# Decision trees: key rows begin at query chunk 22 in place of 26, value rows share every second step with a chunk, leaf weights asked for ahead of slot rows

## The chip, the core and the metric

The kernel runs on one core of a Trainium2 chip. The metric is device time in microseconds; the kernel before takes 2354.35 us, the median of three executions (2353.2 to 2354.74). TensorE (PE in the rows; PEld is its weight load), VectorE (DVE), ScalarE (ACT), GpSimd (POOL) and SyncE (SP) each run their own instructions in order and meet only through semaphores. SyncE issues most DMAs; GpSimd issues the indirect ones.

## What is computed

A decoder of 12 layers over 64 sequences of 64 tokens, 128 features each. The change touches the third layer alone, an attention whose queries, keys and values come out of three decision trees. Each tree has 4 levels and 16 leaves, and each leaf is a small two-layer network (128 to 64 to 128):

```python
def _fff(x, node_w, node_b, w1, b1, w2, b2):
    ...
    cur = jnp.zeros((N,), jnp.int32)
    for _ in range(DEPTH):
        pw = node_w[cur]
        score = jnp.einsum('nd,nd->n', xf, pw) + node_b[cur]
        cur = 2 * cur + 1 + (score >= 0).astype(jnp.int32)
    leaf = cur - N_NODES
    sel = jax.nn.one_hot(leaf, N_LEAVES, dtype=xf.dtype)
    hidden_all = jax.nn.relu(jnp.einsum('nd,ldh->lnh', xf, w1) + b1[:, None, :])
    hidden = hidden_all * sel.T[:, :, None]
    out = jnp.einsum('lnh,lho->no', hidden, w2) + sel @ b2
...
attn = jax.nn.softmax(jnp.einsum('bqd,bkd->bqk', q, k) * scale, axis=-1)
return jnp.einsum('bqk,bkd->bqd', attn, v)
```

## The kernel before

The layer is the function `trees`. Its 4096 tokens are 32 tiles of 128, or 8 groups (`g`) of 512.

**Queries** are computed densely: all 16 leaves for every token, the wrong ones switched off. The work is 64 *chunks*, `m` = 0 to 63: chunk `m` is two leaves of group `m // 8`. `make_hidden(m)` (lines 2057, 2058) makes its hidden part in one of two PSUM banks, ScalarE's `relu` (1948) takes it to SBUF, `add_leaf(m)` (2067) multiplies by the second matrix and sums the group in PSUM; the first chunk of a group also multiplies in the biases (2065). After eight chunks ScalarE takes the group's query (`take_q`, 1952). `turn_leaves(b)` (2032) transposes the leaf choices of two groups; the first is made ahead, the others at chunks given by `leaves_at`.

**Keys and values** are computed sparsely. GpSimd scatters the tokens into a table in memory, sorted by leaf (1742): 32 indirect DMAs for the keys, then 32 for the values. The table has 47 tiles of 128 slots for each, every tile of one leaf. Four tiles make a *quad*; quads 0 to 11 are key rows, 12 to 23 value rows (quads 11 and 23 have three tiles). SyncE loads a quad's slots into one of 5 buffers (`load_slots`, 1692) and the weights of each tile's leaf into one of 16 (`load_weights`, 1685), whose address it reads from a table (1684). For quad `m` TensorE transposes the slots (`turn_rows`, 2078), VectorE copies them (1859), TensorE makes the hidden part (`hide_rows`, 2087), ScalarE takes it with bias and relu (1959), TensorE makes the output (`yield_rows`, 2097), VectorE copies it (1866) and SyncE stores it (`store_rows`, 1698).

GpSimd then fetches the rows back to their tokens with 32 indirect DMAs for keys (1751), four to a group, group 0 once quad 11 is stored, group `g` once the transpose of group `g - 2` is done, and 32 for values (1763), once all quads are stored and all key groups fetched; it waits after every second value group. TensorE transposes the keys of group `g` (`turn_k`, 2105), makes scores (`score`, 2116), VectorE and ScalarE the softmax's numerators, TensorE transposes them (`turn_weights`, 2126) and multiplies by the values (`weigh`, 2140), and VectorE adds the result to x (`update`, 1887). The next layer starts when all engines are done.

**The order** is written out by hand, the same on each engine. Chunks run alone up to a fixed one, `ROWS_FROM`. From there on a counter of steps, `i`, starts at 0, and step `i` holds a chunk as long as there are any, the transpose of quad `i`, the hidden part of quad `i - 1`, the output of quad `i - 2`, and whatever the tables `keys_at`, `scores_at`, `weights_at` and `values_at` place there. On TensorE:

```python
for m in range(LAST + ROWS_FROM + 1):
    i = m - ROWS_FROM
    ...
    if m < NM:
        add_leaf(m)
    if rows_at(i):
        turn_rows(i)
    if rows_at(i - 1):
        hide_rows(i - 1)
    if rows_at(i - 2):
        yield_rows(i - 2)
```

SyncE has its own loop: it loads the weights of quads 0 to 3 and the slots of quads 0 to 4 ahead, and then, in iteration `m`, stores quad `m`, loads the slots of quad `m + 5` and the weights of quad `m + 4`.

## Time and profile before

| what | value |
|---|---|
| time, median of 3 executions | 2354.35 us (2353.2 to 2354.74) |
| span of the profiled execution, first to last instruction | 2356.9 us |
| busy: TensorE, VectorE, ScalarE, GpSimd | 75%, 57%, 47%, 32% of the span |
| the stage `trees` in that execution | 395.9 to 725.6 us; the next layer starts at 729.0 |
| row steps (step 0 to the output of quad 23) | 507.9 to 661.5 us |

The table's three times belong to executions of their own, the span to the profiled one; what lies around the span (start and end of the program) is not in it. The busy shares are means over twelve layers with different limits, and say nothing of this stage; what it waits for is read in its own stretch, engine by engine, since all are in order. Of the rows below, those of a timeline begin with the start and the duration in us, and end, in brackets, with the time that the engine was idle before and what ended it ("remote": a semaphore whose update the profile ties to no instruction close by). "SPq" is SyncE's queue.

### The profile page before, as it was taken

What the parts mean: (1) busy time and instruction counts of PE and PEld (TensorE: products, weight loads), DVE (VectorE), ACT (ScalarE), POOL (GpSimd) and SP (SyncE); (2) the same over time, 40 slices, a digit from 0 to 9 for tenths busy, and PEclk for the clock granted to TensorE, in tenths of its full rate; (3) what the DMA queues carried; (4) which work ended last, traced back from release to release, by engine and by line L of the source; (5) the groups of instructions that cost most, each with busy time, mean ns of one, the idle gap of its engine ahead of it and who ended that gap; (6) DMA issues with size and microseconds to landing.
All of it is one profiled execution on the core that took longest, in us unless ns stands there. A gap on an engine that the chain in (4) does not pass through costs nothing. (4 is left out here: it accounts for less than half of the span.)

```text
span 2356.9 us, 39525 instructions
## 1 busy us (share of the span) xinstructions
PE 1774.8 (75%) x14484; PEld 1215.4 (52%) x14484; DVE 1337.8 (57%) x3646; ACT 1099.5 (47%) x2273; POOL 746.9 (32%) x718
## 2 busy tenths in 40 slices
PE   3887553999895996767999386887788868743994
PEld 1555432435543664644798253565555535542774
DVE  3897587502123774654343365885369969862223
ACT  4775531223243775733344243774357657610441
POOL 1223201360354331146255002330223232165453
PEclk9888885798896998877999697998979969955997
DMA  4111361125623301102376200000000010011224
GB/s 158 83 83 82 104 235 45 49 75 150 161 70 132 124 2 50 37 30 85 110 238 201 75 1 27 28 20 10 3 1 2 2 37 28 11 49 60 62 81 138
DMA packets 145170, 173.18 MB, mean 73 GB/s; under 512 B 21073, under 2 KB 120593, under 8 KB 144049
## 3 DMA queue, kind: packets, MB, share of 16 engines
q1 hardware_dynamic: 125252, 129.09, 17.7%
q0 software_dynamic: 13248, 28.21, 3.6%
q10 hardware_dynamic: 6480, 13.37, 1.5%
q8 instruction: 117, 1.92, 0.3%
q14 instruction: 73, 0.60, 0.1%
HBM read 126.84 MB, written 79.05 MB: 87 GB/s over the span
## 5 line engine op out<-in xcount | busy, mean ns | idle before, releaser
L1154 PE MATMUL a_AV<-a_vx,a_pT 128*64 128x18 f32 (+1 forms) x3072 | 115.1, 224 | 33.0 <-DVE a_two L824 15.3
L1154 PEld LDWEIGHTS a_AV<-a_vx,a_pT 128*64 128x64 f32 x3072 | 105.9, 146 | 62.2 <-issue 28.6
L1016 ACT ACTIVATE a_e<-a_e 128x512 f32<-128x512 f32 x192 | 110.2, 622 | 58.7 <-DVE a_e L846 58.5
L1141 PE MATMUL a_TP<-ident,a_e 128*128 128x128 f32 x768 | 108.0, 285 | 20.0 <-ACT a_e L1016 19.4
L1021 ACT COPY a_pT<-a_TP 128x512 f32<-128x512 f32 x192 | 103.4, 588 | 39.6 <-PE a_TP L1141 39.4
L846 DVE TENSOR_TENSOR a_e<-a_S,a_mx 128x1024 f32<-128x1024 f32 x96 | 117.3, 1222 | 2.9
L1141 PEld LDWEIGHTS a_TP<-ident,a_e 128*128 128x128 f32 x768 | 89.2, 146 | 57.6 <-ACT a_e L1016 48.3
L1130 PE MATMUL a_S<-a_kbd,a_qT 64*64 64x512 f32 x768 | 113.8, 668 | 0.9 <-issue 0.6
L3620 POOL DMA_INDIRECT f_back<-f_ys,f_row x78 | 74.7, 957 | 97.5 <-DVE f_ys L3709 85.6
L3126 POOL DMA_INDIRECT f_back<-f_ys,f_row x80 | 76.6, 957 | 87.1 <-DVE f_ys L3287 66.9
L3759 ACT ACTIVATE f_h<-f_H,f_wt 128x256 f32<-128x256 f32 x156 | 65.2, 473 | 83.5 <-PE f_H L3835 83.5
L843 DVE TENSOR_REDUCE a_mx<-a_S 128x16 f32<-128x1024 f32 x66 | 80.8, 1224 | 40.6 <-PE a_S L1130 39.4
L3352 ACT ACTIVATE f_h<-f_H,f_b 128x512 f32<-128x512 f32 (+1 forms) x96 | 56.5, 615 | 85.4 <-PE f_H L3445 78.6
L1948 ACT ACTIVATE f_h<-f_H,f_b 128x512 f32<-128x512 f32 x64 | 44.0, 687 | 103.1 <-PE f_H L2058 85.5
L1154 PE MATMUL x_AV<-x_vx,x_pT 128*64 128x18 f32 x2048 | 74.2, 215 | 23.7 <-ACT x_pT L1021 17.0
L843 DVE TENSOR_REDUCE x_mx<-x_S 128x16 f32<-128x1024 f32 x64 | 78.1, 1221 | 24.3 <-PE x_S L1130 24.0
L681 POOL TENSOR_TENSOR a_kbd<-a_kT,a_mask 128x512 f32<-128x512 f32 x64 | 64.5, 1039 | 81.1 <-ACT a_kT L991 81.1
L1154 PEld LDWEIGHTS x_AV<-x_vx,x_pT 128*64 128x64 f32 x2048 | 69.0, 142 | 37.2 <-issue 24.9
L1141 PEld LDWEIGHTS x_TP<-ident,x_e 128*128 128x128 f32 x512 | 58.4, 146 | 55.0 <-ACT x_e L1016 45.3
L1141 PE MATMUL x_TP<-ident,x_e 128*128 128x128 f32 x512 | 74.7, 290 | 15.5 <-ACT x_e L1016 15.4
L999 ACT ACTIVATE a_kbd<-a_kT,a_mask 128x512 f32<-128x512 f32 x128 | 85.6, 723 | 0.4
L671 POOL TENSOR_TENSOR a_rstd<-a_var,neghalf 128x4 f32<-128x4 f32 x24 | 24.3, 1014 | 187.7 <-DVE a_var L747 117.8
(544 smaller groups left out, 4731.4 us busy)
## 6 DMA issues: line engine op xcount, KB each, us to landing
f_wt<-in_f_ew SPq DMA_DIRECT2D x39, 584.0 KB
f_slots<-in_blank SPq DMA_DIRECT2D x1, 18576.0 KB
f_wt<-in_f_leaf SPq DMA_DIRECT2D x94, 98.0 KB, 2.0
f_xs<-f_slots SPq DMA_DIRECT2D x47, 144.0 KB
memory_x_k<-w_stage ACTq DMA_DIRECT2D x24, 256.0 KB, 3.2
f_slots<-in_blank SPq DMA_DIRECT2D x1, 5760.0 KB
f_xs<-leaf_slots SPq DMA_DIRECT2D x22, 256.0 KB
leaf_out<-f_ys SPq DMA_DIRECT2D x22, 256.0 KB
```

What stands on the lines that cost most here:

```text
L681: last = pool.tensor_tensor(kbd[:, n % 2, b:b + 2, 0:4, :], bc(kv[:, b:b + 2, :], 2, shape), mask8[:, 0:4].unsqueeze(1).unsqueeze(3).to_br ...
L843: return v.tensor_reduce(mx[:, i % 2, :], unit(i), AX.X, ALU.max)
L846: v.tensor_tensor(e[:, i % 2, :, :], unit(i), bc(mx[:, i % 2, :], 2, [P, NH, SL]), ALU.subtract).then_inc(shifted.sem, 1)
L999: last = act.activation(kbd[:, n % 2, :, h, :], keys(n).rearrange("p (b j) -> p b j", j=SL), ACT.Copy, scale=mask8[:, h:h + 1])
L1016: act.activation(eh, eh, ACT.Exp).then_inc(weights.sem, 1)
L1021: act.copy(pT[:, 4 * n:4 * n + 4, :], TP[:, n, :].rearrange("p (a b) -> p a b", a=4)).then_inc(pT_half.sem, 1)
L1130: last = pe.matmul(S[64 * c:64 * c + 64, i % 2, r, :], qT[rows, g % 2, SL * b:SL * b + SL], kbd[rows, g % 2, b, :, :], start=True, stop=True)
L1141: last = pe.transpose(TP[:, half, P * n:P * n + P], ev[:, 4 * half + n, :], k.ident[:, :])
L1154: last = pe.matmul(AV[64 * c:64 * c + 64, 2 * hp * W1:2 * (hp + 1) * W1], pT[:, hp, 64 * c:64 * c + 64], vx[:, g % 2, t, c, 2 * hp:2 * hp ...
L3126: pool.indirect_dma_start(out=back[:, :], out_offset=bass.IndirectOffsetOnAxis(ap=row[:, i % RR, t:t + 1], axis=0), in_=ys[:, i % RY, t, : ...
L3620: pool.indirect_dma_start(out=back[:, :], out_offset=bass.IndirectOffsetOnAxis(ap=row[:, i % RR, t:t + 1], axis=0), in_=ys[:, i % RY, t, : ...
L3759: act.activation(h[:, i % 2, c, 0:P * n], hid(i, c, n), ACT.Gelu_apprx_tanh, bias=weights(i)[2][:, c:c + 1])\
```

## The change

```diff
-    ROWS_FROM = 26
-    LAST = 46
-    leaves_at = {8: 1, 14: 2, 20: 3}
-    keys_at = {max(16 + 2 * g, 8 * g - 15): g for g in range(NG)}
-    scores_at = {25 + 2 * g if g < NG - 1 else 42: g for g in range(NG)}
-    weights_at = {27 + 2 * g if g < NG - 1 else 44: g for g in range(NG)}
-    values_at = {31 + 2 * g: g for g in range(NG)}
+    ROWS_FROM = 22
+    LAST = 52
+    leaves_at = {6: 1, 11: 2, 16: 3}
+    keys_at = {i: g for g, i in enumerate((17, 19, 21, 23, 24, 26, 34, 42))}
+    scores_at = {i: g for g, i in enumerate((24, 26, 28, 30, 32, 34, 42, 49))}
+    weights_at = {i: g for g, i in enumerate((26, 28, 30, 32, 34, 36, 44, 51))}
+    values_at = {i: g for g, i in enumerate((32, 34, 36, 38, 40, 43, 46, 52))}
     rows_at = lambda m: 0 <= m < 2 * NQ
+
+    def chunk_at(i):
+        if i < NQ:
+            return ROWS_FROM + i
+        if i < 2 * NQ + 2:
+            return None if (i - NQ) % 2 else ROWS_FROM + NQ + (i - NQ) // 2
+        m = ROWS_FROM + NQ + (NQ + 2) // 2 + i - 2 * NQ - 2
+        return m if m < NM else None
...
             for m in range(2 * NQ):
                 store_rows(m)
-                if m + RXS == NQ:
-                    sp.wait_ge(scattered[1].sem, scattered[1].after(NT - 1))
-                if rows_at(m + RXS):
+                if rows_at(m + RXS) and not NQ - RXS <= m < NQ - 3:
+                    if m == NQ - 3:
+                        sp.wait_ge(scattered[1].sem, scattered[1].after(NT - 1))
+                        for n in range(NQ, NQ + RXS - 3):
+                            load_slots(n)
                     load_slots(m + RXS)
```

`NQ` is 12, `RXS` 5 and `NM` 64. The loops of TensorE and ScalarE now run over the step `i` from -22 to 52 and take their chunk from `chunk_at(i)`: chunk `22 + i` up to step 11, chunks 34 to 40 at the even steps 12 to 24, none at the odd steps 13 to 25, and chunks 41 to 63 at steps 26 to 48.

On SyncE, around iterations 7 to 9, before (the store is that of quad 7; the wait for the value scatter is the second semaphore of the slot load):

```order
L1685 DMA f_wt<-in_f_leaf 128x196
L1698 DMA leaf_out<-f_ys 128x4x128 [waits f0_ys_ready]
L1692 DMA f_xs<-leaf_slots 128x4x128 [waits f0_xs_turned,a0_pT_half]
L1684 TENSOR_LOAD f_table [waits f0_ys_out]
L1684 ISA x2
L1685 ISA
L1685 DMA f_wt<-in_f_leaf 128x196
```

and now, from the end of iteration 8 to the first weights of iteration 9:

```order
L1694 DMA f_wt<-in_f_leaf 128x196
L1707 DMA leaf_out<-f_ys 128x4x128 [waits f0_ys_ready]
L1701 DMA f_xs<-leaf_slots 128x4x128 [waits f0_xs_turned,a0_pT_half]
L1701 DMA f_xs<-leaf_slots 128x4x128 [waits f0_xs_turned] x2
L1693 TENSOR_LOAD f_table [waits f0_ys_out]
L1693 ISA x2
L1694 ISA
L1694 DMA f_wt<-in_f_leaf 128x196
```

The wait for the scatter and the slots of quads 12 and 13 have moved behind the store of quad 9, two iterations on; iterations 7 and 8 go from the store straight to the weights.

On TensorE, steps 14 and 15 before (f_H and f_Y are chunks, f_XT, f_HS and f_YS the three parts of the row work):

```order
L2057 MATMUL f_H<-f0w 128x512
L2058 MATMUL f_H<-f_selneg,f_leaf 128x512
L2065 MATMUL f_Y<-moe,f_b 128x512
L2067 MATMUL f_Y<-f_h,f0w 128x512
L2078 MATMUL f_XT<-ident,f_xs 128x128 x4
L2087 MATMUL f_HS<-f_xsT,f_wt 64x128 x4
L2097 MATMUL f_YS<-f_wt,f_hs 128x128 x4
L2057 MATMUL f_H<-f0w 128x512
L2058 MATMUL f_H<-f_selneg,f_leaf 128x512
L2067 MATMUL f_Y<-f_h,f0w 128x512
L2078 MATMUL f_XT<-ident,f_xs 128x128 x4
L2087 MATMUL f_HS<-f_xsT,f_wt 64x128 x4
```

and now:

```order
L2068 MATMUL f_H<-f0w 128x512
L2069 MATMUL f_H<-f_selneg,f_leaf 128x512
L2078 MATMUL f_Y<-f_h,f0w 128x512
L2089 MATMUL f_XT<-ident,f_xs 128x128 x4
L2098 MATMUL f_HS<-f_xsT,f_wt 64x128 x4
L2108 MATMUL f_YS<-f_wt,f_hs 128x128 x4
L2089 MATMUL f_XT<-ident,f_xs 128x128 x4
L2098 MATMUL f_HS<-f_xsT,f_wt 64x128 x4
L2108 MATMUL f_YS<-f_wt,f_hs 128x128 x4
```

Step 15 has lost its chunk, and the row work of two quads stands side by side.

## Rows read from the trace of the kernel before

**Rows 1.** SyncE's queue in the timeline (start us, us, engine line op out<-in xcount)
```profile
536.95 1.48 SPq L1698 DMA_DIRECT2D leaf_out<-f_ys  x1
...
544.16 0.42 SPq L1698 DMA_DIRECT2D leaf_out<-f_ys  x1
...
561.83 0.43 SPq L1698 DMA_DIRECT2D leaf_out<-f_ys  x1
...
567.64 0.43 SPq L1698 DMA_DIRECT2D leaf_out<-f_ys  x1
...
604.82 7.57 SPq L1685 DMA_DIRECT2D f_wt<-in_f_leaf  x4
...
649.91 0.43 SPq L1698 DMA_DIRECT2D leaf_out<-f_ys  x1
```
**Rows 2.** waits of SyncE's queue, 505 to 729 us (us in total, times, longest)
```profile
SPq L1698 <- DVE f_ys L1866: 39.5, 3, 36.0
```
**Rows 3.** timeline of TensorE in one row step ([idle before <-releaser] last)
```profile
555.37 0.60 PE L2078 MATMUL f_XT<-ident,f_xs 128*128 128x128 f32 x4
...
557.91 1.02 PE L2057 MATMUL f_H<-f0w 128*128 128x512 f32 x2
...
560.14 0.60 PE L2078 MATMUL f_XT<-ident,f_xs 128*128 128x128 f32 x4
```
**Rows 4.** timeline of TensorE where it waits for leaf weights
```profile
585.95 0.43 PE L2087 MATMUL f_HS<-f_xsT,f_wt 128*64 128x128 f32 x2 [0.64 <-DMA f_wt<-in_f_leaf]
```
**Rows 5.** timeline of TensorE and of GpSimd, last key groups and first value tile
```profile
664.38 0.60 PE L2105 MATMUL f_PJ<-ident,f_got_k 128*128 128x128 f32 x4
...
672.34 0.94 POOL L1763 DMA_INDIRECT f_xn<-leaf_out,f_slot  x1 [2.40 <-DMA f_got_k<-leaf_out,f_slot]
```
**Rows 6.** timeline of TensorE and of VectorE at the end of the stage
```profile
711.93 1.12 PE L2116 MATMUL f_SC<-moe 128*64 128x64 f32 x16
...
722.31 2.05 PE L2140 MATMUL f_YS<-f_xn,moe 128*128 128x128 f32 x8 [2.88 <-issue]
...
724.47 1.13 DVE L1887 SCALAR_TENSOR_TENSOR x<-f_YS,f_rs,x 128x128 f32<-128x128 f32 x4 [4.48 <-PE f_YS L2140]
```
**Rows 7.** timeline: SyncE's slot loads, TensorE behind chunk 22 and at step 0
```profile
488.56 2.88 SPq L1692 DMA_DIRECT2D f_xs<-leaf_slots  x5
...
498.08 1.02 PE L2057 MATMUL f_H<-f0w 128*128 128x512 f32 x2
...
507.86 0.60 PE L2078 MATMUL f_XT<-ident,f_xs 128*128 128x128 f32 x4
```
**Rows 8.** timeline of TensorE, GpSimd and VectorE while value rows are scattered
```profile
521.11 0.63 PE L2078 MATMUL f_XT<-ident,f_xs 128*128 128x128 f32 x4 [0.27 <-DVE f_xsT L1859]
...
532.11 0.95 POOL L1742 DMA_INDIRECT leaf_slots<-f_xn,f_slot  x1 [0.31 <-issue]
...
535.31 0.69 DVE L1859 COPY f_xsT<-f_XT 128x512 f32<-128x512 f32 x1 [7.83 <-remote]
```
**Rows 9.** instructions of SyncE that read the table of leaves (ns min/median/max)
```profile
L1684 SPq TENSOR_LOAD <-f_table x94: 3/268/873, 444.9 to 652.9; - x94
```
**Rows 10.** timeline of TensorE in the tail, under value fetches
```profile
672.96 0.69 PE L2116 MATMUL f_SC<-moe 128*64 128x64 f32 x16
673.57 0.66 PE L2126 MATMUL f_HS<-ident,f_ebd 128*128 128x128 f32 x4
674.07 1.02 PE L2057 MATMUL f_H<-f0w 128*128 128x512 f32 x2
...
675.25 1.02 PE L2065 MATMUL f_Y<-moe,f_b 32*128 32x512 f32 x2
...
680.59 1.06 PE L2140 MATMUL f_XT<-f_xn,moe 128*128 128x128 f32 x8
...
702.60 1.06 PE L2140 MATMUL f_YS<-f_xn,moe 128*128 128x128 f32 x8
```
**Rows 11.** one window: busy us of PE, PEld, DVE, ACT, POOL; clock; DMA share; GB/s
```profile
528.00:546.00 18.00, 15.77 (x47) 8.60 (x47) 3.08 (x5) 4.79 (x12) 3.84 (x5) 0.54 0.50 135
```

More of the change, by code:

```diff
@@ L1988, in _ @@
             relu(0)
-            for m in range(LAST + ROWS_FROM + 1):
-                i = m - ROWS_FROM
-                if m + 1 < NM:
+            for i in range(-ROWS_FROM, LAST + 1):
+                m = chunk_at(i)
+                if m is not None and m + 1 < NM:
                     relu(m + 1)
@@ L1994, in _ @@
                     take_leaves(leaves_at[m])
-                if m < NM and m % NC == NC - 1:
+                if m is not None and m % NC == NC - 1:
                     take_q(m // NC)
@@ L2158, in _ @@
             make_hidden(0)
-            for m in range(LAST + ROWS_FROM + 1):
-                i = m - ROWS_FROM
-                if m + 1 < NM:
+            for i in range(-ROWS_FROM, LAST + 1):
+                m = chunk_at(i)
+                if m is not None and m + 1 < NM:
                     make_hidden(m + 1)
@@ L2164, in _ @@
                     turn_leaves(leaves_at[m])
-                if m < NM:
+                if m is not None:
                     add_leaf(m)
```

## The prediction

> **What bounds the stage now.** I read the SyncE queue first, then TensorE, then GpSimd, because key and value rows pass through all three. One row block (a quad: four leaf tiles of 128 tokens) costs SyncE one store, one slot load and four leaf-weight loads. In a quiet stretch the store of one quad starts at 561.83 and the next at 567.64, so 5.81 us per quad, and the queue never rests in between [rows 1]. In the whole row stretch SyncE waits for a result three times, 39.5 us together, the longest 36.0 before the first store [rows 2]: behind that it always has work. TensorE needs less. A row step (transpose, hidden, output) and one chunk of the query tree take from 555.37 to 560.14, 4.77 us, of which the chunk is 2.23 (557.91 to 560.14) and the rows 2.54 [rows 3]. So TensorE runs ahead of the queue until it waits for weights, as at 585.95 [rows 4]. The rows are bound by the order SyncE can issue them in: 18 quads from the store at 536.95 (the second) to the one at 649.91 (the twentieth) take 112.96, or 6.28 each; 5.81 each would be 104.6, and the rest lies in stretches like the one at 604.82, where four weight loads take 7.57, more than a whole quad does elsewhere [rows 1].
>
> Behind the rows stands a tail. TensorE turns key group 5 at 664.38, GpSimd fetches the last key group, and then 32 value tiles one by one, the first issued at 672.34 [rows 5]; the last product starts at 722.31 and the last update of x ends at 725.60 [rows 6]. From the store at 649.91 to there it is 75.7 us. In that tail GpSimd is the bound. TensorE stands idle for 2.88 us before that last product, and does little from its scores at 711.93 on [rows 6], since its last chunk is long done.
>
> **The change, part by part.**
>
> *Rows begin four chunks earlier.* Step 0 turns the first slot rows at 507.86, behind chunk 26. The instruction behind chunk 22's last product starts at 498.08 [rows 7], and there the new step 0 stands. That is 9.8 us earlier, and 9.8 is the most this part can give. It needs slot rows in SBUF: the five loads are issued from 488.56 [rows 7]. The least is nothing, for a reason the trace shows. GpSimd scatters value rows until 533.1 (the last begins at 532.11), and while that runs signals from TensorE reach the others late: the transposes of 521.11 last 0.63, and the VectorE copy that waits for them starts at 535.31 [rows 8]. Three row steps pass there where five or six could. The new rows overlap this stretch for 37 us instead of 27, so part of the head start is spent in it. Today the second store is issued 29.1 us after step 0 and the third 36.3 (544.16). Kept at that distance the third would be at 534.4; but the queue is slow in the scatter too: between the first two stores it has one quad to issue and takes until 536.95, and two such quads now lie in the scatter where one does today. I put the third store at 538, a gain of 6, nearer to the full value than to none, as the results of the first two quads come before the scatter ends either way.
>
> *Value rows share every second step with a chunk.* Steps 13, 15, up to 25, seven of them, lose their chunk on TensorE and ScalarE: 7 x 2.23 = 15.6 us of TensorE time. I cost this at nothing gained in the row part, because what hides TensorE there is the queue's 5.81 against 4.77 (with a key transpose, 5.30 on every second step). It can only take up delays: TensorE has 3.3 us of slack in a thin step. A step that stalls today on a late signal no longer delays the queue; today it hardly does either [rows 2].
>
> *Weights ahead of slot rows.* Quads 12 and 13 get their slot load not in iterations 7 and 8 but, with quad 14's, in iteration 9, behind the wait for the scatter, which by then has long ended. The queue's total is the same six DMAs per quad. What is late next is the transpose of quad 12: its load follows the store of quad 9, which TensorE finishes one step before, so TensorE waits there for the whole lag of the queue plus a landing, some 5 us. It waits once, and the queue has weights to issue meanwhile. Cost on the path: bounded by 0 and one quad, 5.8; taken as 0.
>
> One price in the queue also stands in a page. Reading a leaf's address from the table takes 268 ns in the middle [rows 9]. The Trainium skill ("DMA: Bandwidth & Descriptors", Latency and other measured facts) gives a floor of about 600 ns for such a load; by it a quad would cost 1.3 us more and the row part some 24 us more than the rows show, so the trace decides.
>
> *Key groups fetched sooner in fewer instructions' time.* The first fetch still follows the store of quad 11; key transposes move by one step. Two thin steps before the fetch of the last key group save about 1 us there: the value fetch starts some 21 us behind the twentieth store where it is 22.4 now. This helps GpSimd alone.
>
> *Relief.* Key fetches now come with gaps (transposes at 17, 19, 21), where twelve ran nearly together today beside the loads at 604.82. A quad with 7.57 for its weights must lose over 3 us; I count 1.5 of it. Head in sum: 6 + 1.5 = **7.5 us earlier** at the twentieth store.
>
> *The tail.* Chunks 22 to 63 are still to be done, and 19 of them are done by step 25 where today 30 are; behind the row steps 23 remain (steps 26 to 48) in place of 12. TensorE in order, from the twentieth store: today 14.5 to the start of the key transpose at 664.38, past three chunks; now past two, one of them with a bias product (1.0 [rows 10]): 14.5 + 0.53 for the transpose - 2.23 + 0.5 (half of the bias lies in the wait for weights) = 13.3. Then 22 chunks of 2.23, less 1.3 since the last makes no next hidden part: 47.8. Two bias products, 2.0. Six scores at 0.61 and seven transposes of weights at 0.50 (starts at 672.96, 673.57, 674.07 [rows 10]): 7.2. Two key transposes, 1.1. Seven value products at 0.9 (1.06 long with some 0.17 of overlap [rows 10]): 6.3. Together 64.4, so 77.7. Behind the last chunk group 7 has to go through in series: query copied, scores 0.6, shift and exponential, transpose 0.5, copy, product 0.9, update 1.1. Today the scores of that group start at 711.93 and x is done at 725.60 [rows 6], 13.7, waiting for GpSimd; the four named parts alone are 3.1. With some 0.6 to 1.0 for each of the four others I take 6.7. The end is at 84.4 against 75.7. GpSimd's last values land 50.0 behind the first fetch (672.34 to 722.31), thus at 21 + 50 = 71, so **TensorE is the bound of the tail** and not GpSimd, 8.7 us longer. Under fetches TensorE now loses a little: what stands from 672.96 to 703.66 sums to 29.5 by the prices above and takes 30.7 [rows 10]. On 64 us that is 2.6 at most, 0 at least; I take 1.2. Tail in sum: **9.9 later**.
>
> *Moved leaf transposes* (chunks 6, 11, 16) read selections made before chunk 0; nothing.
>
> **Sum:** -7.5 + 9.9 = +2.4 us. The profiled span is 2356.9, 2.5 above the median of the runs, 2354.35. I set the difference on the median: 2356.8, with the span at about 2359.3. A measurement of this kernel can tell about 0.2%, 4.7 us, from no change; +2.4 lies inside.
>
> **Rivals.**
>
> *Slower.* The thin steps leave TensorE idle for over a third of the time, and its granted clock falls after such stretches: it is 0.54 in 528 to 546, behind the stalls [rows 11]. If it is at half when the tail begins, and late signals cost 13 instead of 9.9 now that TensorE is the tail's bound, while the head yields only 5 because the scatter eats it, the result is +8, 2362. It decides as soon as the head gives under 5.2 with the tail as forecast. For it: the tail is on TensorE with no slack, and every lost microsecond counts. Against: the tail begins with 22 dense chunks, and today's dense chunks under the same fetches lose only 4% [rows 10]. Chance 0.30.
>
> *Faster by relief.* All of the excess over 5.81 per quad (8.4 us) comes from TensorE's density beside GpSimd's bursts; thinner steps and the gaps free it, and the full 9.8 is kept: head -15, tail +8.7, -6.3, 2348. For: the slow loads stand only where bursts and row steps meet. Against: the first ones come in the scatter, where nothing is thinned. Chance 0.13.
>
> *Rows bound by TensorE.* If the waits for weights were incidental, the seven chunks would come off the head: -7.5 - 15.6 + 9.9 = -13, 2341. Against it stand the steady 5.81 and SyncE's lack of waits. Chance 0.05.
>
> *Late signals belong to the recording.* Reading one address takes SyncE from 3 to 873 ns [rows 9], so in bursts the queue itself is held up, and not only by partners. If that happens only while they are recorded, timed runs keep the full 9.8, and the tail loses 8.7: -1.1, 2353. For the opposite: the recorded span is only 2.5 above the timed runs. Chance 0.12. The Trainium skill ("NOTIFIC — the notification-queue block", 7.1 Overflow) says that the block's inner path holds producers back rather than lose a record, which would act this way; no run shows it yet.
>
> **The numbers.** Forecast 0.40. Same is forecast and recording, 0.52; slower 0.30; faster 0.13 + 0.05 = 0.18. The range leaves out the case at 2341 and about the outer tenth of the two large rivals: 2347.5 to 2364.
>
> **What would show it.** Step 0 near 498. Third store near 538, twentieth near 642.4, 5.8 apart in quiet stretches with thin and full steps alike; TensorE waiting on weights in nearly every value step, and once on slot rows before quad 12. First value fetch near 663.5. Then TensorE busy almost without gaps to about 720, value products starting well after their rows have landed, the last update near 728. Wrong if value-row stores come under 5.5 apart (rows were TensorE's), if the twentieth store stands before 636 or after 648, or if TensorE waits for values in the tail.

## The result and the profile after

The changed kernel is slower: 2371.48 us, the median of 10 executions (2355.61 to 2375.66), against 2354.55 for the kernel before, run beside it (ten executions, 2345.75 to 2362.88). The ratio is 1.0068, 95% interval 1.0051 to 1.0086, which is 12 to 20 us. It is estimated from all executions, and can differ from the quotient of the medians by up to 0.13% in what follows. I had forecast 2356.8, no measurable change, with a range to 2364. Two later rounds, again with the kernel before beside it, gave 1.0058 (1.0035 to 1.0081) and 1.0056 (1.0036 to 1.0075). Its executions vary by some 20 us, those of the kernel before by 17.

The profiled execution took 2363.1, with this span and these busy times:

```profile
span 2361.3 us, 39525 instructions
PE 1780.1 (75%) x14484; PEld 1220.3 (52%) x14484; DVE 1337.9 (57%) x3646; ACT 1101.8 (47%) x2273; POOL 747.2 (32%) x718
```

That span is 4.4 over the one before. The page says nothing more; the stage has to be read in two halves, up to the twentieth store and behind it.

**The head.** SyncE's queue and TensorE's step 0 in the timeline of the changed kernel:

```profile
512.49 0.36 SPq L1707 DMA_DIRECT2D leaf_out<-f_ys  x1
...
515.36 7.83 SPq L1694 DMA_DIRECT2D f_wt<-in_f_leaf  x4
523.96 0.38 SPq L1707 DMA_DIRECT2D leaf_out<-f_ys  x1
...
526.79 7.10 SPq L1694 DMA_DIRECT2D f_wt<-in_f_leaf  x4
536.15 0.38 SPq L1707 DMA_DIRECT2D leaf_out<-f_ys  x1
...
641.93 0.43 SPq L1707 DMA_DIRECT2D leaf_out<-f_ys  x1
```
```profile
498.32 0.60 PE L2089 MATMUL f_XT<-ident,f_xs 128*128 128x128 f32 x4
```

Step 0 stands at 498.32 against 507.86 [rows 7], as forecast. The third store is at 536.15 against 544.16 [rows 1]: 8.0 earlier where I had put 6. From the third to the twentieth store it is 105.8 us in both. The thin steps (those without a chunk) gave the rows nothing, and the twentieth store is 8.0 earlier, at 641.93. The scatter ate its part as foreseen: two rounds of four weight loads take 7.83 and 7.10 there.

The granted clock of the row part did change. One window, the same columns as [rows 11]; the kernel before first, then the changed one:

```profile
570.00:645.00 75.00, 67.56 (x308) 38.05 (x306) 16.33 (x24) 24.39 (x64) 18.91 (x20) 0.91 0.60 158
```
```profile
570.00:645.00 75.00, 58.15 (x274) 38.08 (x274) 15.50 (x24) 19.50 (x57) 18.91 (x20) 0.79 0.60 162
```

TensorE works 9.4 us less in 75 and is granted 0.79 of full speed instead of 0.91. The row rate did not suffer, which fits the queue as the bound.

Before quad 12 TensorE waits for slot rows, 6.67 us where I expected some 5. The three loads stand behind the store of quad 9, and the next store is late:

```profile
578.41 1.12 PE L2089 MATMUL f_XT<-ident,f_xs 128*128 128x128 f32 x4 [6.67 <-DMA f_xs<-leaf_slots]
```
```profile
565.99 0.43 SPq L1707 DMA_DIRECT2D leaf_out<-f_ys  x1
...
574.71 0.43 SPq L1707 DMA_DIRECT2D leaf_out<-f_ys  x1
575.25 1.72 SPq L1701 DMA_DIRECT2D f_xs<-leaf_slots  x3
...
583.76 0.38 SPq L1707 DMA_DIRECT2D leaf_out<-f_ys  x1
```

The store of quad 10 comes 9.05 behind that of quad 9, but the two quads ahead of it, which load no slots, took 3.8 and 4.9. The three together take 17.8 us, and the same three take 16.4 in the kernel before. So most of the wait is given back, and 1.4 us of it stays.

**The tail.** TensorE, with VectorE's last update:

```profile
656.23 0.60 PE L2116 MATMUL f_PJ<-ident,f_got_k 128*128 128x128 f32 x4
...
661.06 0.38 PE L2069 MATMUL f_H<-f_selneg,f_leaf 32*128 32x512 bf16 x1
665.03 2.07 PE L2078 MATMUL f_Y<-f_h,f0w 128*128 128x512 f32 x2 [3.59 <-ACT f_h L1959]
667.04 1.12 PE L2127 MATMUL f_SC<-moe 128*64 128x64 f32 x16
668.09 0.72 PE L2137 MATMUL f_HS<-ident,f_ebd 128*128 128x128 f32 x4
668.64 1.02 PE L2068 MATMUL f_H<-f0w 128*128 128x512 f32 x2
...
724.23 1.98 PE L2078 MATMUL f_Y<-f_h,f0w 128*128 128x512 f32 x4
726.99 0.69 PE L2127 MATMUL f_SC<-moe 128*64 128x64 f32 x16 [0.78 <-ACT moe L1963]
729.52 0.98 PE L2137 MATMUL f_HS<-ident,f_ebd 128*128 128x128 f32 x4 [1.85 <-ACT f_ebd L1984]
731.23 2.04 PE L2151 MATMUL f_YS<-f_xn,moe 128*128 128x128 f32 x8 [0.72 <-issue]
```
```profile
733.38 1.13 DVE L1898 SCALAR_TENSOR_TENSOR x<-f_YS,f_rs,x 128x128 f32<-128x128 f32 x4 [2.98 <-PE f_YS L2151]
```

From the twentieth store to the last update it is 92.6 us, against 75.7 before [rows 1, 6], and 85.6 forecast. TensorE is the bound, as forecast: it is busy in all of the 55 us from 669 to 724, and GpSimd's last fetch starts at 711.0, 20 us ahead of the last product (3.4 before). The next layer starts at 735.8, 6.7 later than before, not 8.9, because it now follows the last update by 1.3 instead of 3.4.

What the forecast of 85.6 lacks are 7.0 us. The key transpose comes 14.3 behind the store (13.3 said). From there to the end of the last chunk, 724.23 plus 1.98, it is 70.0; my terms had 65.6 with 1.2 for losses. In the gap lies one place: TensorE waits 3.59 us for ScalarE and then works at half clock (granted 0.66 in 664 to 669), so that the three pieces from 665.03 to 668.64 take 3.6 instead of 2.1. That is 5.1 of loss, not 1.2. The last serial part takes 8.3 (6.7 said), its last product 2.04 at half clock where 1.06 is usual [rows 10]; the clock granted in 726 to 734.5 is 0.72.

ScalarE in that gap waited too, and VectorE with it, for results that TensorE had written 4 us and more before (its scores began at 656.76, its transposes at 657.38):

```profile
661.43 0.42 DVE L1882 TENSOR_REDUCE f_mx<-f_SC 128x4 f32<-128x256 f32 x1 [5.95 <-remote]
```
```profile
662.87 0.58 ACT L1989 COPY moe<-f_HS 128x512 f32<-128x512 f32 x1 [5.41 <-remote]
```

This resembles the late signal of [rows 8], now in the tail. GpSimd issues the last two key groups without a pause here, one fetch each 1.25 us from 652.9 to 662.6.

### The profile page after: what moved, and what is told of

It reads as the page before. It is cut to its first block and busy times, and to the rows that moved or that the text cites. A ratio compares the mean times of both kernels' runs of the same rounds, so it can differ in the third digit from the quotient of the medians.

```text
span 2361.3 us, 39525 instructions
## 1 busy us (share of the span) xinstructions
PE 1780.1 (75%) x14484; PEld 1220.3 (52%) x14484; DVE 1337.9 (57%) x3646; ACT 1101.8 (47%) x2273; POOL 747.2 (32%) x718
## 5 line engine op out<-in xcount | busy, mean ns | idle before, releaser
L1154 PEld LDWEIGHTS a_AV<-a_vx,a_pT 128*64 128x64 f32 x3072 | 105.9, 146 | 62.1 <-issue 28.5
L1141 PE MATMUL a_TP<-ident,a_e 128*128 128x128 f32 x768 | 108.1, 285 | 19.9 <-ACT a_e L1016 19.3
L3631 POOL DMA_INDIRECT f_back<-f_ys,f_row x78 | 74.7, 957 | 93.6 <-DVE f_ys L3720 81.7
L999 ACT ACTIVATE a_kbd<-a_kT,a_mask 128x512 f32<-128x512 f32 x128 | 85.6, 723 | 0.4
```

The lines of the kernel that those rows point to most:

```text
L999: last = act.activation(kbd[:, n % 2, :, h, :], keys(n).rearrange("p (b j) -> p b j", j=SL), ACT.Copy, scale=mask8[:, h:h + 1])
L1141: last = pe.transpose(TP[:, half, P * n:P * n + P], ev[:, 4 * half + n, :], k.ident[:, :])
L1154: last = pe.matmul(AV[64 * c:64 * c + 64, 2 * hp * W1:2 * (hp + 1) * W1], pT[:, hp, 64 * c:64 * c + 64], vx[:, g % 2, t, c, 2 * hp:2 * hp ...
L3631: pool.indirect_dma_start(out=back[:, :], out_offset=bass.IndirectOffsetOnAxis(ap=row[:, i % RR, t:t + 1], axis=0), in_=ys[:, i % RY, t, : ...
```

## The experiments

A *thin step* is one without a chunk, a *dense* stretch has a chunk in every step; *head* and *tail* are what lies before and behind the twentieth store. Three checkpoints are compared in the profiles: the first scatter of slot rows (440 to 445), the twentieth store, counted from that scatter, and the tail, from that store to the last update.

| kernel | profiles | twentieth store | tail | time against before (95%) |
|---|---|---|---|---|
| before | 3 | 208.4, 207.8, 201.9 | 75.7, 76.8, 73.1 | 1 |
| changed | 6 | 200.0, 194.9, 202.1, 192.9, 199.7, 194.1 | 92.6, 92.8, 96.5, 90.8, 97.1, 97.0 | 1.0068, 1.0058, 1.0056 |
| early start alone | 1 | 192.8 | 79.9 | 0.9981 (0.9965 to 0.9996) |
| start at 24 | 1 | 198.6 | 76.5 | 0.9987 (0.9965 to 1.0010) |
| early start, new SyncE order | 1 | 195.6 | 77.8 | 0.9969 (0.9950 to 0.9987) |
| changed, chunk in every step | 1 | 195.2 | 88.1 | 1.0018 (1.0002 to 1.0033) |
| thin steps and tables alone | 1 | 199.8 | 87.6 | 1.0036 (1.0019 to 1.0054) |
| changed, old SyncE order | 2 | 199.5, 198.6 | 93.6, 94.4 | 1.0053 (1.0037 to 1.0069), 1.0057 (1.0038 to 1.0076) |
| changed, key group 5 later | 1 | 194.8 | 92.0 | 1.0042 (1.0016 to 1.0069) |
| changed, narrow chunks | 1 | 196.2 | 87.1 | 1.0034 (1.0007 to 1.0060) |

One round (changed, chunk in every step; early start with new SyncE order; the third profile of the changed kernel; the second of the one before) ran on a chip where the kernel before takes 2369.0 instead of 2354. Its times are compared with that alone; the other chips are called the usual ones.

**The changed kernel again.** No edit.

> The changed kernel once more, in nothing altered. Its ten timed runs have a median 16.9 us over the kernel before (2371.5 against 2354.6), while its profiled execution is only 8.5 us over (2363.1), and its ten runs lie between 2355.6 and 2375.7. Theory A (the tail of the trees stage is longer by 17 us from twentieth store to last update, the head gives back 8): the new profile has the last update of x at 734 to 737 us again and whatever is over that is spread over the layers behind, with a lower granted clock (mean 0.847 to 0.854 as in the long runs, 0.858 in the profiled one). Theory B (the stage itself has a good and a bad course, decided by when signals arrive in the scatter): a profile with a span near 2370 has its last update near 744, and TensorE waits more in 510 to 560. Ratio to before again 1.005 to 1.009.

Measured: median 2367.74 of 9 (2353.09 to 2376.19), before 2354.09. The profiled execution was the shortest, 2353.09, with the same tail, 92.8; its last update ends at 727.9, where theory A had 734 to 737. Its gain is ahead of the tail: first scatter 1.7 earlier, twentieth store 5.1 quicker from there. No long execution was caught, so the two theories stayed open on that point.

**The early start alone.**

```diff
-    ROWS_FROM = 26
+    ROWS_FROM = 22
-    leaves_at = {8: 1, 14: 2, 20: 3}
+    leaves_at = {6: 1, 11: 2, 16: 3}
```

> Rows begin at chunk 22 and the leaf transposes are moved; the steps' tables, a chunk in every step and SyncE's order stay as before. Theory A (tail): 16 chunks are left behind step 25 where the kernel before has 12 and the changed one 23; TensorE's work behind the twentieth store is about 15.6 us less than in the changed kernel, so GpSimd bounds the tail again near 76, the twentieth store is 6 to 8 earlier than 649.9, and the time is 6 to 8 below before: 2347 to 2349. Theory C (row steps that fall in the scatter cost TensorE its clock and its signals, and the loss comes back later): the head start is eaten, 2353 to 2360, and the spread of its runs is as wide as the changed kernel's.

Measured: 2348.27 against 2354.09, 5.8 faster, as theory A had it, with a spread of 13 us. SyncE's queue and VectorE's last update, in its timeline:

```profile
513.32 0.36 SPq L1698 DMA_DIRECT2D leaf_out<-f_ys  x1
...
528.54 0.42 SPq L1698 DMA_DIRECT2D leaf_out<-f_ys  x1
...
637.25 0.43 SPq L1698 DMA_DIRECT2D leaf_out<-f_ys  x1
```
```profile
715.99 1.13 DVE L1887 SCALAR_TENSOR_TENSOR x<-f_YS,f_rs,x 128x128 f32<-128x128 f32 x4 [2.05 <-PE f_YS L2140]
```

The tail is 79.9 with four chunks more than before, only 4 longer: most of their 8.9 us goes into time in which TensorE used to wait for GpSimd. Theory A had the total right and both parts too small: a tail near 76, and a twentieth store 6 to 8 earlier than 649.9, where it is 12.7 earlier. So the head start is worth having; row steps in the scatter do not hurt (theory C falls).

**Thin steps, tables and SyncE order, without the early start.** The changed kernel with `ROWS_FROM = 26`.

> Rows begin at chunk 26 as before, but with the changed kernel's step tables, its thin steps 13 to 25 and its SyncE order: 19 chunks are left behind step 25. Theory A (tail): the twentieth store stands at 649 to 651, TensorE has 9 us less in the tail than in the changed kernel, the last update comes 79 to 84 us behind that store, 4 to 8 us over before: 2358 to 2363. Theory C (start in the scatter is what hurts): no loss here beyond the tail, and a spread of runs as before's, 2354 to 2360. Theory D (thin steps leave TensorE idle, the granted clock falls and the layers behind pay): 2363 to 2370 with a mean clock under 0.855.

Measured: 2363.66, 9.6 slower. The tail is 87.6 with 19 chunks behind step 25, over what I had set for A (79 to 84). The twentieth store is at 641.6, where the kernel before has 649.9, 651.7 and 644.9; the third store of this kernel came 28.6 behind step 0, those of before 36.3, 34.5 and 29.2, so the difference lies in the scatter, where this kernel's steps are the same as before's. It is the course of one execution, and my first profile of before was a late one. The time lies just inside what theory D had (2363 to 2370), but its loss behind the stage is not there: from the last update to the end of the program it is 1632.2 us here, and 1631.3 and 1637.5 in the two profiles of before on the usual chips.

**The old order of SyncE.** The changed kernel with the slot loads of quads 12 and 13 in iterations 7 and 8, measured twice, the second time beside the changed kernel:

```diff
-                if rows_at(m + RXS) and not NQ - RXS <= m < NQ - 3:
-                    if m == NQ - 3:
-                        sp.wait_ge(scattered[1].sem, scattered[1].after(NT - 1))
-                        for n in range(NQ, NQ + RXS - 3):
-                            load_slots(n)
+                if m + RXS == NQ:
+                    sp.wait_ge(scattered[1].sem, scattered[1].after(NT - 1))
+                if rows_at(m + RXS):
```

> The changed kernel with SyncE's order of before (slot rows of quads 12 and 13 loaded in iterations 7 and 8, not all in iteration 9). Theory A (tail): the 6.7 us for which TensorE waits for slot rows before quad 12 goes, SyncE loses nothing by it or 2 us at most, the twentieth store comes at 639 to 642 and the time is 0 to 3 below the changed kernel's. Theory E (that wait is what drops TensorE's clock to half at 578 us and starts the late steps behind it): the twentieth store comes before 638 and the time is 6 or more below the changed kernel's. If the scatter of value rows holds SyncE up in the new place, it is slower than the changed kernel.

> The changed kernel with SyncE's old order, again, beside the changed kernel on the same chip. Their medians were 2364.8 and 2369.5, while the same edit on the dense kernel changed nothing (0.9981 and 0.9969 of the kernel before). Theory E (the wait for slot rows costs in the thin kernel): again 3 to 6 below the changed kernel. Theory A (covered by the lag of the queue): within 2 of it.

> The changed kernel beside the others of this job, as the partner of the kernel with SyncE's old order. Over the kernel before by 13 to 17 us, tail 92 to 97.

Measured: 2364.81 the first time, 2367.37 the second, and beside it the changed kernel 2366.27. The first gap of 3 to 5 did not come again. Twentieth store and tail are as in the changed kernel. Only the stretch from the third to the twentieth store is shorter, 104.8 in both profiles, against 105.5 to 105.9 in the three of the changed kernel whose third store is as late: the 1 us that the wait leaves, far below what the times can show.

**The new order of SyncE on the early start.** The same block, put into the early start alone.

> The early start alone (measured 2348.3) with the changed kernel's SyncE order added. Theory E (the wait of TensorE for slot rows before quad 12 delays the rows, for which the changed kernel's 2369.5 over 19 runs against 2364.8 with the old order speaks): 3 to 6 over it, 2351 to 2354, with a wait of 5 to 7 us on slot rows at step 12 and a twentieth store 3 to 5 us later. Theory A: that wait is covered by the lag of the queue, the time stays at 2347 to 2350.

Measured: 2363.26 on the slower chip, 0.9969 of before: by its time theory A again. Its TensorE does wait:

```profile
572.03 1.12 PE L2080 MATMUL f_XT<-ident,f_xs 128*128 128x128 f32 x4 [6.26 <-DMA f_xs<-leaf_slots]
```

6.26 us of idle TensorE on the way to the twentieth store, and nothing in the time. From the third to the twentieth store it is 112.0 here and 108.7 in the early start alone, near what theory E had for the rows (3 to 5); the tail is 2.1 shorter. With one profile of each, on two chips, that decides nothing. "Leaf weights ahead of slot rows" is neutral within the 0.2% or so that these times can tell.

**A chunk in every step.** The changed kernel, with this in place of its `chunk_at`:

```diff
+    def chunk_at(i):
+        m = ROWS_FROM + i
+        return m if m < NM else None
```

> The changed kernel with its start at chunk 22, its step tables and its SyncE order, but with a chunk in every step. Theory A (the seven chunks taken out of the thin steps are paid for in the tail): 16 chunks are left behind step 25, the tail from twentieth store to last update is 78 to 82 as in the kernel with the early start alone (79.9) in place of 92.6 to 93.6, and the time is 12 to 17 below the changed kernel's: 2352 to 2358. Theory F (the step tables, with key, score and value work late in the program, hold up the tail): it stays above 2362. TensorE's granted clock in 570 to 645 is at half for about 34 us in the changed kernel's profile and 14 in the early start alone; by theory A it is near 14 to 20 here.

Measured: 2373.87 against 2369.03, 4.8 slower, which would be 2359 where before takes 2354: between theory A (2352 to 2358) and F (over 2362). Filling the thin steps takes away some 10 of the 12 to 17 us, but not all. The granted clock in 570 to 645 is back at 0.87, 19.5 us at half, as A had it; the tail is 88.1, not 80. The reason is in the tables. The end of TensorE's timeline here, then that of the early start with the new SyncE order, which differs in the tables only:

```profile
705.34 1.02 PE L2074 MATMUL f_Y<-f_h,f0w 128*128 128x512 f32 x2
...
706.73 0.69 PE L2123 MATMUL f_SC<-moe 128*64 128x64 f32 x16
...
715.40 2.04 PE L2147 MATMUL f_XT<-f_xn,moe 128*128 128x128 f32 x8 [3.26 <-issue]
717.37 1.12 PE L2123 MATMUL f_SC<-moe 128*64 128x64 f32 x16
720.39 1.12 PE L2133 MATMUL f_HS<-ident,f_ebd 128*128 128x128 f32 x4 [1.90 <-ACT f_ebd L1980]
722.23 2.05 PE L2147 MATMUL f_YS<-f_xn,moe 128*128 128x128 f32 x8 [0.72 <-issue]
```
```profile
701.88 1.98 PE L2069 MATMUL f_Y<-f_h,f0w 128*128 128x512 f32 x4
...
705.12 0.69 PE L2118 MATMUL f_SC<-moe 128*64 128x64 f32 x16
...
711.44 1.12 PE L2128 MATMUL f_HS<-ident,f_ebd 128*128 128x128 f32 x4 [4.54 <-ACT f_ebd L1975]
713.27 2.05 PE L2142 MATMUL f_YS<-f_xn,moe 128*128 128x128 f32 x8 [0.72 <-issue]
```

The changed tables score group 6 at step 42 and group 7 at step 49, behind group 6's values. With chunks up to step 48 that order is right; with the last chunk at step 41 nothing stands between, and the two groups go through softmax one behind the other: 705.12 to the end is 11.4 us in the one, 706.73 to the end 18.8 in the other. So theory F's mechanism holds for this kernel, but not for the changed one, in which scoring group 7 waits for its last chunk. Thin steps and tables belong together, 7 chunks moved behind the rows and an order that fits; their joint price is the step from 0.9969 to some 1.006, about 21 us. How it divides between the two is not shown.

**Key group 5 later.**

```diff
-    keys_at = {i: g for g, i in enumerate((17, 19, 21, 23, 24, 26, 34, 42))}
+    keys_at = {i: g for g, i in enumerate((17, 19, 21, 23, 24, 28, 34, 42))}
```

> The changed kernel with one entry of its tables moved: the transpose of key group 5 at step 28 in place of 26. In every profile with the changed tables TensorE turns key group 4 and 5 within 4 us, so GpSimd fetches the last two key groups in one piece (eight fetches, 652.9 to 662.6), and behind it TensorE waits 3.6 to 4.2 us for ScalarE and then runs some 3.4 us at half clock. In the kernel before there are 1.7 us between the two groups and no such wait. Theory G (the unbroken burst of eight makes signals late): with 4.5 us between the two groups the wait of 3.6 goes or is under 1, the tail is 87 to 90 in place of 92.6 to 93.6, the time 3 to 6 below the changed kernel of this job. Rival (the wait belongs to the place in ScalarE's order, between scores and weights): the wait stays where it is, 3 to 4 us, and so does the time. GpSimd's value fetches begin 4 to 5 us later, without cost, since TensorE bounds that tail.

Measured: 2362.81, beside the changed kernel's 2366.27; the intervals overlap, so this decides nothing. In the profile the wait of 3.6 at that place is gone, and another has come, on TensorE, before the first value product:

```profile
671.01 1.16 PE L2151 MATMUL f_XT<-f_xn,moe 128*128 128x128 f32 x8 [2.22 <-issue]
672.01 1.76 PE L2068 MATMUL f_H<-f0w 128*128 128x512 f32 x2
```

Half clock from there to 677.8. The tail is 92.0. Breaking the burst removes the wait at that place, as theory G has it; that it saves time is not shown, and a wait came elsewhere. That the bursts themselves make the signals late is argued from this one pair and from the count at the end of this document.

**The start at chunk 24**, otherwise the early start alone.

> The early start alone, with the start at chunk 24 in place of 22: 14 chunks left behind step 25. Theory A (head and tail as sums): the start is 4.9 later than at 22 and the tail 1 to 3 shorter (77 to 78, GpSimd bounds it), so 1 to 4 above the start at 22 and 2 to 5 below the kernel before. If row steps in the scatter are what costs, it is as fast as the start at 22 or faster.

Measured: 2350.22 against 2354.43, the twentieth store 5.8 later than with the start at 22, the tail 3.4 shorter. About as theory A has it (4.9, and 1 to 3), though the interval includes no change.

**Less work in the tail.** The last twelve chunks of the changed kernel over 128 of 512 columns; three quarters of the queries of groups 6 and 7 are left out:

```diff
-                pe.matmul(H[:, m % 2, :], w1[:, c, :], xT(g), start=True, stop=False)
-                pe.matmul(H[:, m % 2, :], leaf[:, c, :].bitcast(BF16), selneg[:, g, :], start=False, stop=True).then_inc(hidden.sem, 1)
+                w = GN if m < NM - 12 or m == NM - 8 else P
+                pe.matmul(H[:, m % 2, 0:w], w1[:, c, :], xT(g)[:, 0:w], start=True, stop=False)
+                pe.matmul(H[:, m % 2, 0:w], leaf[:, c, :].bitcast(BF16), selneg[:, g, 0:w], start=False, stop=True).then_inc(hidden.sem, 1)
...
-                ins = pe.matmul(Y[:, :], w2[:, c, :], h[:, m % 2, :], start=False, stop=c == NC - 1)
+                w = GN if m < NM - 12 or c == NC - 1 else P
+                ins = pe.matmul(Y[:, 0:w], w2[:, c, :], h[:, m % 2, 0:w], start=False, stop=c == NC - 1)
```

> The changed kernel, whose last twelve chunks (52 to 63) do their three products over 128 of the 512 columns only, except the output product of each group's eighth chunk; so the queries of groups 6 and 7 are computed for a quarter of their tokens only, and the output is not the reference's. Everything else, SyncE's and GpSimd's work and all waits, is as in the changed kernel. TensorE's work there falls from 2.23 us per chunk to 0.6 to 1.0 (ScalarE's 0.69 between the products may bound it), 15 to 18 us in all. Theory A (TensorE's chunks are the tail): the tail falls from 93 until GpSimd bounds it, whose last values land 6.7 before the last update in the kernel before: 78 to 83, and the time is 10 to 15 below the changed kernel's, near the kernel before or under it. Theory D (the loss is behind the stage): the tail may fall, but the time stays 6 or more over the kernel before.

Measured: 2358.53, 1.0034 of before: by the ratios some 5 to 8 below the changed kernel, and a tail of 87.1. I had set 10 to 15, and 78 to 83. The median stands in a gap: six of the twelve executions take 2349.7 to 2355.7, six 2361.3 to 2374.0, and the profiled one (2352.95) is of the first six. Three rows of TensorE's timeline show why:

```profile
661.45 2.07 PE L2080 MATMUL f_Y<-f_h,f0w 128*128 128x512 f32 x2 [4.15 <-ACT f_h L1959]
...
690.58 0.38 PE L2069 MATMUL f_H<-f0w 128*128 128x128 f32 x2
...
716.62 0.69 PE L2129 MATMUL f_SC<-moe 128*64 128x64 f32 x16 [0.78 <-ACT moe L1963]
```

From the first narrow chunk to the scores of group 7 it takes 26.0 us where the changed kernel takes 36.0 (690.96 to 726.99). So 10 us come off, not 15 to 18; in that stretch TensorE waits three times for ScalarE's relu, which still takes 0.69, 3.3 us in all. This execution lost 4 us more ahead of that, at the wait of 4.15 and behind it. That about half of the loss goes with 10 us of TensorE's work fits theory A better than D. Behind the stage nothing is seen to be lost: from the last update to the end of the program it is 1626.9 us here, 1623.4 to 1635.3 in the changed kernel's five profiles on the usual chips, 1631.3 and 1637.5 in the two of before.

**More profiles of both kernels**, no edit.

> The changed kernel once more, one look. Its two profiles so far are 2363.1 and 2353.1, its median 2369.5. By theory A the tail is 92 to 94 again whatever the total, and the profiles differ only in the head (third store 31 to 38 us behind step 0) and in the layers behind. By theory B a profile over 2367 has a longer tail, or a third store over 40 us behind step 0.

> The kernel before once more, one look, to see which of its profile's numbers are its own and which the course of one execution. Tail from twentieth store to last update 75 to 77 as in the first; the third store 28 to 37 us behind step 0 (36.3 in the first profile, 28.6 in the thin steps alone, which start at the same step 0), so the twentieth store anywhere from 641 to 651.

> The changed kernel, one look. Checkpoints so far in four profiles, from the first scatter of slot rows: step 0 at 52.6 to 56.4, twentieth store at 192.8 to 202.1, tail 90.8 to 96.5. Theory A: tail 90 to 97 again, and the head makes most of the spread between the totals. Theory B: the profiles so far were good draws of the head, and this one has the twentieth store beyond 205.

> As changed_fifth, one more look: tail 90 to 97, twentieth store 193 to 203 behind the first scatter by theory A; beyond 205 by theory B.

> The kernel before, one look. In its two profiles the twentieth store is 208.4 and 207.8 behind the first scatter of slot rows and the tail 75.7 and 76.8. If those two heads were bad draws, this one is under 204; the tail is 75 to 77 again.

Measured, in the order of the texts above: 2382.65 and 2368.48 on the slower chip; 2367.63, 2370.95 and 2357.22 on the other. The table has their checkpoints. Over all profiles the tail is 75.2 on average before and 94.5 after, 19 us longer, and no two values of the two kernels overlap. The twentieth store is 206.0 before and 197.3 after, 8.7 earlier, with a spread of 9 us within one kernel. The gain is in by the third store, 10.1 us on average; from there to the twentieth it is 106.1 before and 107.5 after. None of the changed kernel's six is beyond 205, so theory B falls as to the head. As to the tail it does not: B had a longer tail in executions over 2367, A the same whatever the total, and the three profiles over 2367 have 96.5, 97.1 and 97.0, the three shorter ones 92.6, 92.8 and 90.8. One of the three is from the slower chip, so this is a hint from six. What TensorE waited for ScalarE's relu in the tails of the fifth profile of the changed kernel (first row) and of the sixth (second), from 642 to 741:

```profile
PE f_Y L2078 <- ACT f_h L1959: 6.5, 3, 4.1
```
```profile
PE f_Y L2078 <- ACT f_h L1959: 2.1, 1, 2.1
```

Both have a tail of 97. In the first it lost to waits; in the second TensorE was already at half clock when the tail began:

```profile
642.00:652.00 10.00, 10.00 (x26) 5.05 (x25) 0.42 (x1) 2.14 (x5) 3.78 (x4) 0.50 0.26 76
```

## Why the prediction was wrong

*Step 0 at 498, third store 538, twentieth 642.4:* right (498.3, 536.2, 641.9), the last in part by luck: the third store gained 8.0 instead of 6, and the 1.5 of relief did not come. The head gained 8.0 in the first pair of profiles and 8.7 over all, against 7.5.

*Seven chunks taken out of value steps give the rows nothing:* right. From the third to the twentieth store it is 105.8 us in both kernels of the first pair, so the rival "rows bound by TensorE" falls, and up to that store no value quad of that profile came under 5.8.

*Relief, 1.5 us:* not there. All of the gain is in by the third store. The rival "faster by relief" falls with it.

*Slot rows of quads 12 and 13 in iteration 9, cost 0:* right as far as the times of two pairs of kernels can tell. The wait is 6.7, not 5, and by the stores 1 to 1.4 us of it stays in the changed kernel.

*TensorE becomes the bound of the tail:* right, and there the loss is. *The tail, 9.9 longer:* this is the step that failed, by its size: 16.9 in the first pair, 19.3 over all profiles. The sum of TensorE's pieces at full clock was good to about 1 us. What was wrong is the term for losses under fetches, "2.6 at most", with 1.2 taken. I had read it from 672.96 to 703.66 in the kernel before [rows 10], and summed that stretch wrongly. It holds seven chunks at 2.23, one bias product at 1.0, five scores at 0.61, five transposes of weights at 0.50, four value products at 0.9 and a key transpose at 0.53: 26.3 us, not 29.5. So 4.4 of its 30.7 are loss, not 1.2, and TensorE does stop in it for ScalarE, with half clock behind:

```profile
693.67 1.12 PE L2067 MATMUL f_Y<-f_h,f0w 128*128 128x512 f32 x2 [1.62 <-ACT f_h L1948]
...
696.57 1.90 PE L2140 MATMUL f_XT<-f_xn,moe 128*128 128x128 f32 x8
```

The second profile of before has 4.31 at such a wait of its tail, the third 1.49. At the rate of that stretch the 64.4 us of the new tail lose 10.8, an estimate, which was the bound to take in place of 2.6; with it the sum is +12, 2366, outside the range that I gave. Measured, the changed kernel's first profile has 3.6 us of waiting and 1.5 of half clock, others up to 8.0 of waiting for ScalarE, or half clock carried over from the thin steps. The serial end (6.7 said, 8.3 measured) was taken at full clock; it has waits of 0.78, 1.85 and 0.72 us, and its last product runs at half. Of the 7.0 us that the first profile has over the forecast, 3.9 are this term, 1.6 the serial end and 1.0 the late key transpose.

*The rival "slower", +8:* the right mechanism, on both counts that it names (late signals and half clock in a tail without slack), but with 13 for the tail where it was 17 to 19. So the range ended too low. Its argument against itself, that dense chunks under the same fetches lose only 4%, is the same wrong sum: it is 4.4 on 26.3, or 17%.

*"Late signals belong to the recording":* its forecast, 2353, did not come. Whether signals are late only while an execution is recorded is not tested: every timed execution of the changed kernel has its own span and granted clock on record, and the profiled ones are among them, so none is known to have run unrecorded. The Trainium skill ("NOTIFIC — the notification-queue block", 7.1 Overflow) offers such holding back of producers; whether it makes the signals late when an execution is recorded is neither shown nor excluded here.

*The Trainium skill's floor for reading an address* ("DMA: Bandwidth & Descriptors", Latency and other measured facts): the changed kernel's reads again take 268 ns in the middle, and the trace stays the one to count with.

```profile
L1693 SPq TENSOR_LOAD <-f_table x94: 3/268/722, 445.3 to 644.6; - x94
```

*What stays open.* The stage accounts for 19 minus 9, less 2 at the next layer's start: 8 to 9 us. The changed kernel's five profiled executions on the usual chips average 2363.7, 9.5 over the median of before. Their spans average 2361.9, only 5.7 over the two profiled ones of before there (2356.9 and 2355.5), which were longer than that kernel's median. The median of its 29 timed executions there, these five among them, is 2367.8, 13.6 over. So 4 us or more are not placed. That the profiles over 2367 have tails 4 to 5 us longer than the others would account for most of it, but six profiles do not show it. Its mean granted clock is lower in long executions (0.847 at 2375.7, 0.858 at 2355.6), which may be cause or effect.

Two versions beat both kernels: the early start alone (0.9981) and with the new SyncE order (0.9969). What costs is the thin steps together with the tables that go with them.

## What to carry to other kernels

Work taken off an engine where another is the bound is not saved but moved: ask where it lands, and whether the engine is the bound there. Seven chunks worth 15.6 us were hidden in the row part and fully exposed behind it; four others, left to the tail by the early start, cost 4 us for 8.9 of work, since TensorE had slack there. When an engine becomes the bound of a stretch, its losses count in full. Read them from like surroundings by summing every piece at full clock and taking all of the rest as loss (here 4.4 in 30.7, which I had read as 1.2), find the waits that make up the rest, and price the serial end at the clock that its waits leave.

## What the runs showed of the hardware

- TensorE's granted clock in 570 to 645 us was 0.91 to 0.95 in three profiles of before, 0.93 with the early start alone, 0.75 to 0.82 in six profiles of the changed kernel and 0.77 in the thin steps alone. In the sixth profile of the changed kernel it was still 0.50 in 642 to 652, at the beginning of the dense tail.
- Late signals are not bound to the scatter. Nine profiles have eight key fetches of GpSimd in one piece at the beginning of the tail, and in all nine TensorE waits 2.7 to 4.2 us for ScalarE behind it. The kernel with a chunk in every step has its eight in one piece one group earlier, from 642.2, and waits 3.6 behind them. The two with the changed tables in which a pause of 2.4 and 4.7 us divides the eight (the sixth profile, key group 5 later) have no such wait there.
- The kernel before takes 2354 us in four rounds and 2369 in the one on another chip; the changed kernel's single execution there was 13.6 over it, its medians elsewhere 11.8 to 16.9.
- Executions of one kernel can be 7 us and more apart at one checkpoint: the kernel before had its third store 36.3, 34.5 and 29.2 us behind step 0 in three of them, the changed kernel 27.8 to 39.8 in six.
